# A graph layer in split fp32: the first steps in another order, the row sums turned by VectorE, and the DMA queue's order changed

## What is computed

```python
HW  = einsum('bnf,rfo->rbno', h, W[:, :F]) + einsum('rd,rdo->ro', W_edges, W[:, F:])[:, None, None, :]
AHW = einsum('rbnm,rbmo->rbno', A, HW)
out = x + max(AHW, axis=0) + b
```

## Time and profile before

| | us |
|---|---|
| median of 3 runs (218.24 to 221.85) | 219.56 |
| the profiled execution: its time | 219.25 |
| its span, first to last instruction | 217.4 |

### The profile page before, as it was taken

How to read it: one execution, slowest core, us unless ns; L and a number is a source line. 1 busy time by engine, 2 the same in 40 slices (tenths; PEclk the granted TensorE clock), 3 DMA queues, 4 the chain that set the end, 5 groups by cost and what they waited for, 6 DMA issues and landing times.

```text
span 217.4 us, 4978 instructions
## 1 busy us (share of the span) xinstructions
PE 204.7 (94%) x1013; PEld 166.7 (77%) x1013; DVE 188.7 (87%) x399; ACT 186.5 (86%) x469; POOL 172.6 (79%) x182
## 2 busy tenths in 40 slices
PE   6399989999999999999999999999999999999980
PEld 4378767788888888888888888888888888888860
DVE  3495869999899989999899989999899989979783
ACT  2847979999999999999999999999999999999550
POOL 1743687979889797979889797979989797979341
PEclk9969999999999999999999999999999999999999
DMA  6695957987897987979898997989897997362726
GB/s 234 195 333 136 188 90 225 223 257 171 187 251 140 307 158 259 195 207 235 174 250 147 294 172 250 195 233 217 174 267 137 307 161 269 75 154 38 165 34 91
DMA packets 120320, 42.38 MB, mean 195 GB/s; under 512 B 100743, under 2 KB 110071, under 8 KB 120311
## 3 DMA queue, kind: packets, MB, share of 16 engines
q1 hardware_dynamic: 118688, 41.57, 78.7%
q10 hardware_dynamic: 1623, 0.71, 1.2%
HBM read 38.00 MB, written 4.26 MB: 194 GB/s over the span
## 4 chain that ended last, share of the span: by engine, by line
PE 84%; ACT 4%; DVE 3%; issue 3%; DMA 2%; POOL 2%; SPq 0%; DVEq 0%; ACTq 0%; POOLq 0%
PE rel_ps L845 11%; PE rel_ps L847 11%; PE rel_ps L846 11%; PE at_ps L819 8%; PE bwd_ps L845 7%; PE bwd_ps L847 7%; PE bwd_ps L846 7%; PE fwd_ps L845 6%; PE fwd_ps L847 6%; PE fwd_ps L846 6%; PE turn_ps L830 3%; DMA a_sb<-in_adj 2%; ACT h_sb L463 1%; DVE best L671 1%; ACT a_hi L440 1%
## 5 line engine op out<-in xcount | busy, mean ns | idle before, releaser
L351 POOL TENSOR_TENSOR a_lo<-a_sb,a_hi 128x512 fp32r<-128x512 f32 x63 | 81.9, 1321 | 18.7 <-ACT a_hi L440 18.7
L493 ACT ACTIVATE rel_ps<-sum_all,c_col 128x512 f32<-128x512 f32 (+1 forms) x63 | 41.6, 673 | 5.2 <-DVE best L671 4.5
L671 DVE TENSOR_TENSOR best<-rel_ps,best 128x512 f32<-128x512 f32 x62 | 42.4, 684 | 3.4 <-PE rel_ps L847 2.3
L440 ACT ACTIVATE a_hi<-a_sb 128x512 fp32r<-128x512 f32 x64 | 39.6, 634 | 3.7 <-DMA a_sb<-in_adj 3.7
L642 DVE TENSOR_TENSOR at_lo<-at_ps,at_hi 128x512 fp32r<-128x512 f32 x48 | 32.7, 685 | 2.5 <-ACT at_hi L453 1.5
L453 ACT ACTIVATE at_hi<-at_ps 128x512 fp32r<-128x512 f32 x48 | 28.3, 590 | 3.3 <-PE at_ps L819 3.2
L845 PE MATMUL bwd_ps<-a_hi,h_hi 128*128 128x512 f32 x64 | 27.2, 425 | 3.3 <-issue 3.3
L366 POOL TENSOR_TENSOR xb_sb<-xp_sb,bias_sb 128x512 f32<-128x512 f32 x16 | 23.1, 1445 | 5.1 <-DMA xp_sb<-in_x 5.1
L845 PE MATMUL fwd_ps<-at_hi,h_hi 128*128 128x512 f32 x64 | 26.7, 417 | 0.0
L847 PE MATMUL bwd_ps<-a_hi,h_lo 128*128 128x512 f32 x64 | 25.7, 402 | 0.0
L846 PE MATMUL bwd_ps<-a_lo,h_hi 128*128 128x512 f32 x64 | 25.6, 399 | 0.0
(11 more groups left out here) (105 smaller groups left out, 471.8 us busy)
## 6 DMA issues: line engine op xcount, KB each, us to landing
a_sb<-in_adj SPq DMA_DIRECT2D x28, 512.0 KB, 4.1
sum_all<-sums_dram SPq DMA_DIRECT2D x16, 512.0 KB, 5.9
x_sb<-in_x SPq DMA_DIRECT2D x16, 256.0 KB, 5.3
xp_sb<-in_x SPq DMA_DIRECT2D x64, 64.0 KB, 2.8
out<-o_sb SPq DMA_DIRECT2D x60, 64.0 KB, 5.1
a_blocks<-in_adj SPq DMA_DIRECT2D x56, 64.0 KB, 2.3
a_sb<-in_adj SPq DMA_DIRECT2D x6, 256.0 KB, 4.7
a_sb<-in_adj ACTq DMA_DIRECT2D x2, 256.0 KB, 3.9
```

Of the source, the lines that this page charges most:

```text
L351: pool.tensor_tensor(a_lo[q][:, j, :], a_sb[q][:, j, :], a_hi[q][:, j, :].bitcast(fp32), ALU.subtract).then_inc(a_lo_ready[j], 1)
L440: act.activation(a_hi[q][:, j, :], a_sb[q][:, j, :], ACT.Copy, accum_out=sums[q][:, 0, j:j + 1]).then_inc(a_hi_ready[j], 1)
L493: act.activation(to[:, cols], sum_all[q][:, 0 if r in FWD else 1, cols], ACT.Copy, scale=c_col[:, r:r + 1]).then_inc(after_it, 1)
L671: dve.tensor_tensor(best[q][:], held[:], best[q][:], ALU.max).then_inc(joined[r], 1)
```

## The change

1. *First steps.* Chunks 0 and 2 of A of batch 0 come by ACT's queue, 1 and 3 by SP's. ACT rounds chunks 0 and 1 of A, then makes h, then rounds chunks 2 and 3. DVE splits chunk 1 of A as well as chunk 0; POOL is left with two. PE does `fwd` 0 ahead of `bwd` 3, and turns A of batch 1 ahead of `fwd` 1. ACT rounds the turned A of batch 1 ahead of its h.
2. *The sums.* `sums` is now 128x32 (24 columns zeroed once by POOL). DVE transposes it by blocks of 32x32 straight in SBUF. PE's `turn_sums`, ACT's `take_sums` and the waits for them are gone. The eight rows of a block of 32 nodes now lie in four groups of partitions, so the store is four DMAs of 8x32 instead of one of 8x128.
3. *SP's queue* is: x, x by blocks, sums, blocks of A, spread, A, result.

```diff
             def store_sums(k, q):
                 sp.wait_ge(sum_rows_ready, 2 * k + q + 1)
-                sp.dma_start(sums_dram[q][:, :], sum_rows[q][:]).then_inc(sums_stored[q], 16)
+                for g in range(G):
+                    sp.dma_start(sums_dram[q][:, g * Q:(g + 1) * Q],
+                                 sum_rows[q][g * Q:g * Q + S, :]).then_inc(sums_stored[q], 16)
...
             def first_steps():
                 load_x(0, 0)
-                load_a(0, 0, 0)
-                load_a(0, 0, 2)
+                load_a(0, 0, 1)
+                load_a(0, 0, 3)
...
                 load_xp(0, 0)
-                load_a_blocks(1, 1)
                 load_xp(0, 1)
                 store_sums(0, 1)
+                load_a_blocks(1, 1)
+                spread_sums(0, 1)
                 reload_a(0, 1)
-                spread_sums(0, 1)
...
                 if more:
                     reload_x(k, q)
                     load_xp(k, q)
-                    load_a_blocks(k + 1, q)
                 store_sums(k, q)
                 if more:
+                    load_a_blocks(k + 1, q)
+                spread_sums(k, q)
+                if more:
                     reload_a(k, q)
-                spread_sums(k, q)
...
-            for j in range(C):
-                round_a(0, 0, j)
+            round_a(0, 0, 0)
+            round_a(0, 0, 1)
             act.wait_ge(x_loaded[0], 16)
             act.wait_ge(shift_ready, 1)
             for j in range(C):
                 normalise_chunk(j)
+            round_a(0, 0, 2)
+            round_a(0, 0, 3)
...
+            def turn_sums(k, q):
+                b = 2 * k + q
+                dve.wait_ge(a_hi_ready[C - 1], b + 1)
+                dve.wait_ge(at_hi_ready[C - 1], b + 1)
+                wait(dve, sums_stored[q], G * 16 * k)
+                dve.transpose(sum_rows[q][:], sums[q][:]).then_inc(sum_rows_ready, 1)
...
                 if not is_batch(b, 1):
                     split_at(k, q, 2)
                     split_at(k, q, 3)
+                    turn_sums(k, q)
                 split_bwd(*prev)
...
                     round_h(*ahead)
+                if is_batch(b, 1):
+                    turn_sums(k, q)
                 join(*prev, FWD[1])
```

More of the change, by code:

```diff
@@ L93, in gnn_layer @@
         shift = pair(sb, "shift", [P, C])
-        sums = pair(sb, "sums", [P, 2, C])
-        sum_rows = pair(sb, "sum_rows", [S, P])
+        sums = pair(sb, "sums", [P, Q])
+        sum_rows = pair(sb, "sum_rows", [P, Q])
         sum_all = pair(sb, "sum_all", [P, 2, N])
@@ L413, in _ @@
             pool.memset(eps[:], EPS)
+            for q in range(2):
+                pool.memset(sums[q][:], 0.0)
             pool.memset(minus_one[:], -1.0).then_inc(consts_ready, 1)
@@ L438, in round_a @@
                 wait(act, bwd_done, b - 1)
-                wait(act, sums_turned, b - 1)
+                wait(act, sum_rows_ready, b - 1)
                 act.activation(a_hi[q][:, j, :], a_sb[q][:, j, :], ACT.Copy,
-                               accum_out=sums[q][:, 0, j:j + 1]).then_inc(a_hi_ready[j], 1)
+                               accum_out=sums[q][:, j:j + 1]).then_inc(a_hi_ready[j], 1)
             def round_at(k, q, i):
@@ L451, in round_at @@
                 wait(act, fwd_done, b - 1)
-                wait(act, sums_turned, b - 1)
+                wait(act, sum_rows_ready, b - 1)
                 act.activation(at_hi[q][:, i, :], at_from(b, i)[:], ACT.Copy,
-                               accum_out=sums[q][:, 1, i:i + 1]).then_inc(at_hi_ready[i], 1)
+                               accum_out=sums[q][:, C + i:C + i + 1]).then_inc(at_hi_ready[i], 1)
             def normalise(k, q):
@@ L483, in round_bwd @@
                 act.activation(bwd_hi[:], bwd_ps[:], ACT.Copy).then_inc(bwd_hi_ready, 1)
-            def take_sums(k, q, turned_ps=turn_ps):
-                act.wait_ge(sums_turned, 2 * k + q + 1)
-                wait(act, sums_stored[q], 16 * k)
-                act.activation(sum_rows[q][:], turned_ps[0:S, 0:P], ACT.Copy).then_inc(sum_rows_ready, 1)
             def fill(k, q, r, to, after_it, cols=slice(0, N)):
@@ L510, in first_step @@
                 round_w(slice(0, W_EYE))
-                take_sums(0, 0, rel_ps[1])
-                normalise(*ahead)
                 round_at(*ahead, 0)
                 round_at(*ahead, 1)
+                normalise(*ahead)
                 round_fwd(0, 0)
@@ L533, in step @@
                 join_first(k, q)
-                if not second:
-                    take_sums(k, q)
                 if second:
@@ L553, in step @@
                     round_at(*ahead, 0)
-                    if second:
-                        take_sums(k, q, rel_ps[1])
                 else:
@@ L570, in _ @@
             act.activation(neg_mean[1][:], minus_one[:], ACT.Copy)
-            for j in (1, 3):
+            for j in (0, 2):
                 act.dma_start(a_sb[0][:, j, :], adj[0, j * P:(j + 1) * P, :]).then_inc(a_loaded[0][j], 16)
@@ L685, in first_step @@
                                   ALU.mult).then_inc(wedge_cols_ready, 1)
-                round_h(*ahead)
                 split_at(*ahead, 0)
@@ L690, in first_step @@
                 dve.tensor_copy(c_col[:], turn_ps[:, 0:R]).then_inc(c_ready, 1)
+                moments(1, 0)
+                round_h(*ahead)
                 split_fwd(0, 0)
-                moments(1, 0)
                 dve.wait_ge(bn_done, 3)
@@ L778, in _ @@
                 split_at(0, 0, i)
+            turn_sums(0, 0)
             split_ht(0, 0)
@@ L825, in turn_h @@
                 wait(pe, ht_lo_ready, b)
-                if not any(is_batch(b, n) for n in range(3)):
-                    pe.wait_ge(sum_rows_ready, b)
                 for j in range(C):
@@ L831, in turn_h @@
                 last.then_inc(h_turned, 1)
-            def turn_sums(k, q, to=turn_ps):
-                b = 2 * k + q
-                pe.wait_ge(a_hi_ready[C - 1], b + 1)
-                pe.wait_ge(at_hi_ready[C - 1], b + 1)
-                if is_batch(b, 0):
-                    pe.wait_ge(at_lo_ready[1], 1)
-                else:
-                    pe.wait_ge(ht_lo_ready, b + 1)
-                pe.transpose(to[0:S, 0:P], sums[q][:].rearrange("p t c -> p (t c)"), ident[:]).then_inc(sums_turned, 1)
             def passes(out, w_hi_, w_lo_, m_hi, m_lo, start, stop, onto=False):
@@ L923, in first_step @@
                 bwd(0, 0, 2)
+                fwd(0, 0, 0)
                 bwd(0, 0, 3)
-                fwd(0, 0, 0)
-                turn_sums(0, 0, rel_ps[1])
-                fwd(0, 0, 1)
                 turn_a(*ahead, 0)
                 turn_a(*ahead, 1)
+                fwd(0, 0, 1)
                 fwd(0, 0, 2)
@@ L951, in step @@
                 fwd(k, q, 1)
-                if not is_batch(b, 1):
-                    turn_sums(k, q)
                 eye(k, q, EYE[1])
```

11 lines of the change are left out of this document (3 added, 8 removed).

## The result

The changed kernel takes 231.8 us (median of 4 runs, 231.1 to 234.3) against 218.9 for the kernel before, measured beside it: a ratio of 1.063, 95% interval 1.057 to 1.069. It is slower by 13 us; the forecast was 215.2, with a range up to 218.0. The profiled execution after has a span of 230.0 us (before 217.4). In what follows a profiled execution that took over 1.5% longer than the fastest run of its kernel (those of a_order, a_one_order and a_room_one) shows the order of events but not the kernel's time, and such runs, with one of b_order at 1156 us, are in the medians but not in the ratios.

A forecast was written before the change was run, and what follows sets the result against it. PE alone was taken to pace the loop, at 12.27 us a batch. Gains and costs of 3.7 − 0.15 + 1.54 − 0.3 − 0.4 = 4.4 us led to a forecast of 215.2 us, range 213.2 to 218.0.

The forecast's parts named there:

- SP's queue: In SP's queue, three more issues per batch take about 1 us of SP's time; the loop's spread still goes out on time.
- The order of the queue: In the loop, sums go ahead of the blocks, whose 1.99 us of issuing cover the landing; the spread goes out unchanged.
- The first steps, 3.7 us: At the start, PE begins sooner and keeps its clock, so `eye` 0 and the last wait come 3.7 us earlier.
- The 1.71 us for the clock: At the start, PE's clock stays up instead of falling to 0.50, giving back half of 3.42 us, 1.71.
- The sums leave PE, 1.54 us: In the loop, PE no longer turns the sums, 0.11 us per batch over 14 batches: 1.54 us gained.
- VectorE's transpose: On DVE, a 128x32 transpose per batch takes 0.15 us and fits its free 0.84; batch 1's costs 0.15.
- Batch 1, −0.3: Batch 1's spread, issued near 32.5, lands at 37.3 where ACT wants it at 37.0: 0.3 us lost, up to 1.5.
- the last batch, −0.4: In the last batch the spread goes out 1.7 us later, costing 0.4 us at the end, between 0 and 1.2.
- the stores land late: In the loop, sums stored as 32 rows of 128 bytes land late, so every batch pays: slower; chance 0.06.
- 237 and 224.6: Times for late-landing stores of the sums: 237 at 1.6 us per batch, 224.6 for a milder 0.7; chance 0.06.

The follow-up runs named there:

- a_order: The changed kernel with the old order of SP's queue and its four stores of the sums: 230.7 us, ratio 1.049.
- a_one_order: The changed kernel with one store of the sums instead of four and SP's queue in the old order: 218.6 us, ratio 0.995.
- a_room_one: The changed kernel with one store of the sums, the loop's old queue order, and x by blocks moved behind the spread: 226.0 us, ratio 1.023.
- b_order: The kernel before with the new order of SP's queue, its one store of the sums kept: 221.6 us, ratio 1.012.
- b_four: The kernel before with its store of the sums cut into four DMAs of 8x32, nothing else changed: 231.2 us, ratio 1.059.
- b_idle_front: The kernel before with three idle 8x32 stores per batch on SP's queue, directly ahead of the store of the sums: 229.2 us, ratio 1.049.
- a_one: The changed kernel with the four stores of the sums made one DMA of 128 rows: 222.5 us, ratio 1.017.
- b_first: The kernel before with the new first steps alone: 216.6 us, ratio 0.990.
- b_dve: The kernel before with the sums turned by VectorE and stored in one piece, first steps and SP's queue as before: 220.8 us, ratio 1.012.
- b_idle: The kernel before with three idle 8x32 stores per batch on SP's queue, behind the spread: 219.5 us, ratio 1.001.
- b_two: The kernel before with its store of the sums cut in two: 222.5 us, four runs between 219.7 and 224.5, no interval.
- a_one_act_order: The changed kernel with one store of the sums, issued on ACT's queue, and SP's queue in the old order: 216.7 us, ratio 0.989.
- a_act: The changed kernel with its four stores of the sums issued on ACT's queue instead of SP's: 229.7 us, ratio 1.049.

## Why the prediction was wrong

**The step that failed is SP's queue**, in the words of the prediction: "Three more issues per batch ... are about 1 us of SP's time"; "In the loop the sums go ahead of the blocks, whose 1.99 us of issuing cover the landing; so the spread goes out when it did". The size was right: 1.39 to 1.48 us for four stores against 0.39 for one, 1.0 us more. What was missing was that SP had no microsecond to give, only 0.1 to 0.3 us a batch. I had compared the batch of 12.27 us with the busy times of four engines and the share of the DMA engines, and SP's queue stands in neither. In the timeline of the kernel before, its round of 12.19 us nearly fills the batch; I had read it only at the places of the sums. The 1.0 us went into the serial stretch of every batch, and the spread, ACT and PE behind it followed: that is shown by b_four (+11.7 us with this edit alone), b_idle_front (+9.8 with idle issues at this place) and a_one (−9 us when three of the four go). The parts measured alone, 11.7 for the issues, 2.1 for the order, 1.3 for the sums on VectorE and −2.7 for the first steps, come to 12.4 us, against 12.9 measured together; they need not add up so well.

**The order of the queue** was said to be free, since the spread goes out when it did. It costs 2.1 us alone (b_order, 0.4 to 4.7), by a held stretch of 7.64 instead of 7.10 (7.66 and 7.75 in the other two kernels that have this order). That the spread ahead of A, not behind it, does this is what the rows suggest; no run tries that edit alone.

**The first steps, 3.7 us.** The working held at every point of it. In the profiled executions the last wait of the start came 3.54 us sooner. Measured alone it is 2.7 us (b_first), a term too large by 1 us, and the traces show three reasons. Not every execution of the old first steps loses its clock: seven profiled executions have these steps, and in 12 to 16 us the granted clock is 0.61 to 0.70 in four (before, b_four, b_order, b_dve) and 1.00 in three (b_idle, b_idle_front, b_two). The 1.71 us for the clock was priced as if it were always lost. Then the execution that the prediction read had the latest start of the seven: its first `bwd` stands at 11.37, the others' at 10.19 to 11.16, since chunk 0 of A landed late (ACT starts on it at 5.99, in the others at 4.81 to 5.78). One trace was taken for the kernel. And in b_first PE waits 0.88 us at 38.20, behind the spread of batch 1, which does not come sooner by as much as PE does.

**The sums leave PE, 1.54 us** (14 x 0.11). Where SP's queue doesn't interfere, a batch is (191.15 − 57.12) / 11 = 12.18 us (a_one_order, the rows below; a_one_act_order has 12.18 too), so 0.09 is gained per batch, 1.2 us in all, near what was said.

```profile
57.12 1.04 PE L827 MATMUL at_ps<-ident,a_sb 128*128 128x128 f32 x8
...
191.15 1.03 PE L827 MATMUL at_ps<-ident,a_sb 128*128 128x128 f32 x8
```

VectorE's transpose took 0.20 us (0.15 said), and it did fit into its room. But what this edit costs elsewhere was priced at 0.4 us (the last batch). With one store on SP's queue the loop gains nothing and the end is 1.5 us longer (b_dve, a net loss of 1.3 us), by a slower store and a wait of 2.43 us. With that store on ACT's queue the loop gains its 1.1 us, but behind the last of the transposes shown the end takes 27.50 us instead of 26.50 (a_one_act_order), so the sums on VectorE bring nothing there either: 216.7 us against b_first's 216.6.

**Batch 1, −0.3, and the last batch, −0.4.** ACT waited for the spread of batch 1 until 37.75 (37.3 said) and PE behind it 0.78 us until 38.50: so of the 3.54 us won at the start 2.78 were left at the first eight transposes, a cost of 0.8, within the 1.5 allowed. The last batch can't be told from the waits of every batch; the whole end behind the last of the transposes shown took 0.73 us more than before.

**The rival "the stores land late"** named the right symptom, the spread later than ACT's need and every batch paying, with a chance of 0.06, and the wrong mechanism. SP waited for stored sums 3.8 us in all, in 3 places (before 3.5, in 7):

```profile
SPq L267 <- DMA sums_dram<-sum_rows: 3.8, 3, 1.5
```

The Trainium skill, DMA: Bandwidth & Descriptors, section "Specifications", with its 512 B for line rate, had spoken against this edit. In the loop of the changed kernel the trace shows nothing of it: the pieces of 128 bytes are in place before SP comes to the spread. In a_act, where ACT issues them while SP is already issuing the blocks, SP does wait for them, but off the path. Where a store is waited for at once, the one of 128 rows is 0.7 us later than the one of 8, as above; that is 128 rows against 8 and doesn't tell the size of a piece from their number.

Of the prices of the rivals, 237 and 224.6 start from the 219.25 of the profiled execution and the others from 219.56; the 0.3 changes nothing.

## To carry to other kernels

A queue that issues DMAs is an engine with a round of its own: lay one round of it beside the batch, with its gaps, before adding an issue to it, because the table of busy times doesn't show it. In this kernel's round the place counted more than the number: small issues in the stretch ahead of the large transfers cost their full time, small ones behind them, where the queue is held back anyway, cost nothing, and large ones moved there cost more than they had ahead. And an event at the start that some executions have and others not, such as the fall of the clock here, is priced from several traces. An edit that takes 0.1 us per batch from the bound and adds 1 us to a neighbour should be judged by the neighbour.

## What had not been expected

- One issue of x (256 KB) took 0.39 to 0.41 us of SP's time where nothing held it back and mostly 1.3 to 2.9 us behind A and the spread; four issues of the result took 2.0 to 5.6 us.
- The held stretch of 7.0 to 7.1 us in the old order hardly changed when 1 us of small issues was added within it or ahead of it (b_idle, b_idle_front, b_four: 7.05, 7.11, 7.03).
- The same four small stores cost ACT 1.2 us of waiting a batch, little less than the 1.4 they took on SP, so moving issues to a busy engine's queue moves the price with them.
